# A causal attention layer solved block by block: the solve moved to the natural layout, with side work placed in the change of tiles

## The reference

```python
logits = jnp.einsum('bhqd,bhkd->bhqk', q, k) * scale
causal_mask = jnp.triu(jnp.full((s, s), -jnp.inf, dtype=logits.dtype), 1)
probs = jax.nn.softmax(logits + causal_mask, axis=-1)
L = jnp.eye(s, dtype=probs.dtype) - jnp.tril(probs, -1)
rhs = jnp.diagonal(probs, axis1=-2, axis2=-1)[..., None] * v
A = jax.scipy.linalg.solve_triangular(L, rhs, lower=True)
attn_output = A.transpose(0, 2, 1, 3).reshape(b, s, HID)
return attn_output @ Wd.T + bd
```

## Time and profile before

| what | us |
|---|---|
| median of 3 runs | 1500.24 (1497.93 to 1505.37) |
| profiled execution, its own span | 1507.1 |
| the steady part of the causal layer, solving 16 tiles | 462 (from 719 to 1181) |
| PE, DVE, ACT, POOL busy in these 462 us | 410, 232, 182, 147 |
| granted TensorE clock in these 462 us, mean | 0.87 |

### The profile page before, as it was taken

One profiled execution on the slowest core, in us unless ns is written; L12 is line 12 of the kernel. 1 busy time (PEld: TensorE's weight loads), 2 busy tenths in 40 slices (PEclk: granted clock), 3 DMA queues, 4 the chain that ended last, 5 costly groups with the idle time before them and its releaser, 6 DMA issues. The chain is left out here.

```text
span 1507.1 us, 30851 instructions
## 1 busy us (share of the span) xinstructions
PE 1237.4 (82%) x11642; PEld 673.8 (45%) x11642; DVE 1035.0 (69%) x2290; ACT 729.2 (48%) x1596; POOL 628.0 (42%) x838
## 2 busy tenths in 40 slices
PE   6656677779999988538889988988988799999976
PEld 2212232222333337424666766666666333333276
DVE  6699999979888955457446646645632588988653
ACT  3834334317766675313524523533442166676754
POOL 2279888853424215314423423223332524351244
PEclk9878888869999998758889879978997599999988
DMA  5378833023224022441421231141120231331213
GB/s 166 145 274 320 298 139 140 20 67 87 55 65 122 13 82 63 100 86 23 88 38 25 45 74 28 21 100 18 18 51 10 67 79 31 97 89 45 81 48 88
DMA packets 137737, 128.41 MB, mean 85 GB/s; under 512 B 92007, under 2 KB 123559, under 8 KB 132202
## 3 DMA queue, kind: packets, MB, share of 16 engines
q1 hardware_dynamic: 129536, 118.56, 28.6%
q0 software_dynamic: 2496, 5.13, 1.1%
q10 hardware_dynamic: 5558, 2.76, 0.9%
HBM read 105.61 MB, written 38.62 MB: 96 GB/s over the span
## 5 line engine op out<-in xcount | busy, mean ns | idle before, releaser
L1393 DVE TENSOR_REDUCE f_row_min<-f_ps 128x1 f32<-128x512 f32 x512 | 323.9, 676 | 55.6 <-PE f_ps L1720 55.2
L1283 ACT ACTIVATE f_e<-f_ps 128x512 f32<-128x512 f32 x512 | 282.8, 602 | 126.4 <-PE f_ps L1740 122.5
L1720 PE MATMUL f_ps<-f_operands 72*128 72x512 bf16 x512 | 205.4, 410 | 26.4 <-DMA f_operands<-k_scr 15.4
L1740 PE MATMUL f_ps<-f_operands 75*128 75x512 bf16 x512 | 189.5, 380 | 2.6 <-ACT f_e L1283 2.1
L790 PE MATMUL m_ps<-m_shared,sb_ident 128*128 128x512 f32 x256 | 136.8, 683 | 58.1 <-DVE m_shared L630 58.0
L363 POOL TENSOR_TENSOR m_drive<-m_du,m_ring 128x1024 f32<-128x1024 f32 x64 | 149.7, 2352 | 56.2 <-DVE m_ps L622 37.6
L495 ACT ACTIVATE m_ps<-m_delta,m_A 128x511 f32<-128x511 f32 x128 | 83.0, 681 | 131.7 <-DVE m_ps L622 109.0
L1751 PE MATMUL f_ps<-f_e,f_v_op 128*32 128x512 f32 x1024 | 136.4, 604 | 2.1 <-ACT f_e L1283 1.4
L2714 DVE TENSOR_TENSOR d_aT<-d_ps,d_aT 128x16 f32<-128x16 f32 x224 | 37.9, 169 | 140.9 <-PE d_ps L2892 140.7
L1720 PEld LDWEIGHTS f_ps<-f_operands 72*128 72x128 bf16 x512 | 51.3, 101 | 181.2 <-DVE f_row_min L1393 127.3
L2545 DVE TENSOR_REDUCE d_row_min<-d_ps 128x1 f32<-128x384 f32 (+3 forms) x176 | 106.3, 634 | 35.9 <-PE d_ps L2786 34.7
(11 more groups left out here) (298 smaller groups left out, 2345.3 us busy)
## 6 DMA issues: line engine op xcount, KB each, us to landing
m_ring<-bc_scr SPq DMA_DIRECT2D x32, 1024.0 KB, 5.4
f_rows_scr<-blank SPq DMA_DIRECT2D x2, 8707.5 KB, 30.8
f_wall<-f_wall SPq DMA_DIRECT2D x16, 578.0 KB
f_operands<-q_scr SPq DMA_DIRECT2D x32, 288.0 KB
f_operands<-k_scr SPq DMA_DIRECT2D x96, 96.0 KB
d_q_op<-q_scr SPq DMA_DIRECT2D x6, 576.0 KB
d_k_op<-k_scr SPq DMA_DIRECT2D x18, 192.0 KB
f_operands<-f_rows_scr SPq DMA_DIRECT2D x46, 64.5 KB, 1.8
```

The source lines that it names most:

```text
L1283: nc.scalar.activation(e_sb[:, n % 3, hh, :], ps[:, SCORE[(b * UNITS + u) % SCORE_BANKS], :], ACT.Exp, scale=SCALE).then_inc(s["e_out"], 1)
L1393: nc.vector.tensor_reduce(row_min[:, b % 2, u // TPB, u % TPB:u % TPB + 1], ps[:, MAXQ[(b * UNITS + u) % MAX_BANKS], :], AX.X, ALU.max, ne ...
L1720: nc.tensor.matmul(ps[:, MAXQ[n % MAX_BANKS], :], q_op(b, QK)[:, hd, t * P:(t + 1) * P], k_op(b, QK)[:, hd, :], start=True, stop=True).the ...
L1740: nc.tensor.matmul(ps[:, SCORE[n % SCORE_BANKS], :], k_op(b, QKS)[:, hd, t * P:(t + 1) * P], q_op(b, QKS)[:, hd, :], start=True, stop=True ...
```

## The change

All of it is in `delta_phase` and the two arrays it loads.

- **Natural layout.** The solution is held in `a_all` with tokens on partitions from the first product on. `product` now takes 32 columns of `mT` as the stationary operand and 8 columns of `a_all` as the moving one, and writes to `ps[own, ...]` with `own = token_group(k)`, one set of 32 PSUM partitions for all eight heads. For an odd k, where the block is the second of its group of 32 tokens, only the 16 rows of the block before are multiplied, and DVE multiplies by a column of zeros and ones (`second`) while it adds. `added` adds 32 x 64 numbers to `a_all` in place. The transposes of `aT` and ACT's copies into `a_nat` between steps are gone; one pair is left after `inverse` (`natural`, and ACT's `turned`).
- **The output** of a tile, two matmuls with `aT` before, is now a copy to `a_flat` (ACT), a transpose (`turn_out`, PE), a copy to `a_out` (ACT) and one matmul (L2938 in the changed kernel).
- **Side work.** Pieces 0 to 3 stand in the change of tiles. Pieces 4 to 13 follow ten of the 14 half-steps. After the half-steps (0, 1), (0, 2), (0, 4) and (0, 6) nothing stands.
- `mT` is computed for 112 of its 128 columns, since the first block needs none.

```diff
-PADDED = NH * HEAD_COLS + 2 * HD
+PADDED = HD + NH * HEAD_COLS
+CHANGE_HOOKS = 4
+HALF_STEPS = [(half, k) for k in range(1, BLKS) for half in range(2)]
+FOLLOWED = [i for i, (half, k) in enumerate(HALF_STEPS) if half or k not in (1, 2, 4, 6)]
+HOOK_AFTER = {i: CHANGE_HOOKS + place for place, i in enumerate(FOLLOWED)}
...
+        def token_group(k):
+            return slice(k // 2 * 2 * BLK, (k // 2 + 1) * 2 * BLK)
...
@@ multiplied, ACT @@
-                    nc.scalar.copy(mT[:, n % 2, i * GROUP:(i + 1) * GROUP, :].rearrange("p h i -> p (h i)"),
-                                   act_bank("mt", n, i)).then_inc(s["act_out"], 1)
+                    nc.scalar.copy(mT[:, n % 2, i * GROUP:(i + 1) * GROUP, BLK:P],
+                                   act_bank("mt", n, i).rearrange("p (h i) -> p h i", h=GROUP)[:, :, BLK:P]).then_inc(s["act_out"], 1)
+
+                def flattened(n):
+                    act.wait_ge(s["at_sb"], 2 * BLKS * (n + 1))
+                    if n >= 1:
+                        act.wait_ge(s["act_out"], in_act("turned_out", n - 1))
+                    nc.scalar.copy(a_flat[:, :, :], every_own(a_all[:, n % TPB, :])).then_inc(s["flat_out"], 1)
...
@@ added, DVE @@
-                    own = slice(k * BLK, (k + 1) * BLK)
+                    rows = token_group(k)
+                    held = own_cols(a_all[rows, n % TPB, :], half)
                     dve.wait_ge(s["at_ps"], 2 * (n * BLKS + k) + half + 1)
-                    nc.vector.tensor_tensor(aT[:, n % 2, half, own], ps[:, STEP[half], own], aT[:, n % 2, half, own],
-                                            ALU.add).then_inc(s["at_sb"], 1)
+                    if k % 2 == 0:
+                        nc.vector.tensor_tensor(held, step_cols(half, rows), held, ALU.add).then_inc(s["at_sb"], 1)
+                    else:
+                        nc.vector.scalar_tensor_tensor(out=held, in0=step_cols(half, rows), scalar=vec(core, "second")[rows, :],
+                                                       in1=held, op0=ALU.mult, op1=ALU.add).then_inc(s["at_sb"], 1)
...
@@ PE @@
                 def product(n, half, k):
-                    pe.wait_ge(s["an_sb"], 2 * (n * BLKS + k - 1) + half + 1)
-                    own = slice(k * BLK, (k + 1) * BLK)
-                    rows = slice(0, k * BLK)
-                    side_by_side(half, a_nat[:, :], lambda hd: mT[rows, n % 2, hd, own], rows, own, s["at_ps"])
-
-                def turned(n, half, k):
-                    pe.wait_ge(s["at_sb"], 2 * (n * BLKS + k) + half + 1)
-                    if n >= 1 and k == 0:
-                        pe.wait_ge(s["an_sb"], 2 * BLKS * n - 1 + half)
-                    turn_half(half, aT[:, n % 2], s["an_ps"])
+                    if k == 1:
+                        pe.wait_ge(s["an_sb"], 2 * n + half + 1)
+                    else:
+                        pe.wait_ge(s["at_sb"], 2 * (n * BLKS + k - 1) + half + 1)
+                    own = token_group(k)
+                    rows = slice(0, own.start) if k % 2 == 0 else slice(own.start, own.start + BLK)
+                    for gl in range(2):
+                        for hh in range(GROUP):
+                            c = (gl * GROUP + hh) * HD
+                            last = nc.tensor.matmul(ps[own, STEP[half], c:c + HD], mT[rows, n % 2, head(half, gl, hh), own],
+                                                    own_dims(a_all[rows, n % TPB, :], head(half, gl, hh)), start=True, stop=True)
+                    last.then_inc(s["at_ps"], 1)
...
+                    for i, (half, k) in enumerate(HALF_STEPS):
+                        product(n, half, k)
+                        if i in HOOK_AFTER:
+                            beside(n, HOOK_AFTER[i])
```

## The result

The changed kernel takes 1614.3 us (median of 4 runs, 1612.6 to 1618.1) against 1500.7 for the kernel before (1497.9 to 1505.4): 1.073 times as long, interval 1.069 to 1.078. The forecast was 1514 and its range ended at 1550. The direction was right and the size wrong by 100 us.

What follows compares the result with a forecast made beforehand. PE was taken to bound the stage, busy 410 of 462 us. Terms of 100 - 7 - 49 - 13 - 11 - 4 - 4 - 3 + 1 + 1 + 6 gave +17, said as +14 on 1500.2: 1514 us, range 1474 to 1550.

Steps and rivals of the forecast that it cites:

- The product: Products on PE: all 16 instructions in one column group, 0.38 us more each at fast clock, 0.64 at slow: +100 us.
- Transposes, waits, output: On PE, 208 transposes go (-49 us), with them the wait for DVE's addition (-13); two output matmuls become one (-4).
- the change of tiles: Between tiles, pieces 0 to 3 stand between PE's transposes of gT and aT, so waits go: -11 us.
- Waits for additions: Sign that the forecast is right: PE's waits for DVE's additions in the stage fall under 8 us.
- mT: The mT matmuls on PE, 112 of 128 columns in 64 groups: between -8 and 0 us, taken as -4.
- The clock: PE's granted clock may rise later in seven cold tiles, two mT groups each: half of 12 us taken, +6.
- the mean clock below 0.80: Sign for the clock case: PE's mean granted clock over the stage, 0.87 before, falls below 0.80.
- Those by tile: Signs in tile lengths: tile 7 about 27 us, tiles 2, 6 and 10 shorter by one to three, 5 and 9 longer.
- the clock stays down: Rival: PE's lighter work holds the clock at 0.5 for another 60 us, +28 or so, 1543 us; chance 0.17.
- priced "at nothing": In the product, the moving operand's fall from 16 columns to 8 was taken to change no time; weights count.
- 225 for both: DVE's addition after each product was to grow from 0.169 us to 0.225, mostly hidden behind PE: +1 us.

Runs made afterwards that it cites:

- filler: Two useless bf16 matmuls of 384 columns ahead of each product, results read by nobody: kernel before 1530.6 us, changed kernel 1633.3 us.

## Why the prediction was wrong

**The product** (+100): the unit prices were right, 0.60 and 0.96 us with starts 0.033 us apart. The total, +96.5 us over 14 tiles, is near by luck. I had 58 of 224 half-steps at half clock and it was 143; the pairs and the vanished waits made up for it.

**Transposes, waits, output** (-49, -13, -4) **and the change of tiles** (-11): right together, -64.4 us over 14 tiles. Waits for additions are under 1 us on PE where I said under 8. Taking the four pieces back cost 9 to 14 us, at overlapping intervals.

**mT** (-4): the sign was wrong, +39.8 us over 14 tiles, through the clock. Nor did the columns save anything: in tile 7 at full clock, with filler in both kernels, the four mT groups hold PE for 3.8 us with 112 columns and for 3.7 with 128.

**The clock** (+6): the step that failed. I priced it as two mT groups in each of seven tiles that were cold already, and held that the side work of the fast tiles would keep them at 1.00. Tile 7 fell to 0.70, and time at half clock rose by some 265 us, from 123 to 389. With all other terms as priced, this one should have been about +100; the estimate from tiles at equal clock puts it at some 77 or more. Of the prediction's signs, the mean clock below 0.80 is the one that came. Those by tile can't be read, since the ends of the stretches moved; from gathering to gathering tile 2, which was to be shorter, is 9 us longer. The rival "the clock stays down" named the mechanism and its point (fast tiles fall too), and was sized at 60 us more of half clock, 28 us of time. Why the clock stays down for so long, 15.4 us in tile 6 with PE never idle, no run takes apart.

What I had in hand and did not use: a moving operand of 8 columns in place of 16 was priced "at nothing". For the product's own length that is right, and in the old layout with one column group it cost 40 us (1579 to 1619) elsewhere. The length of the product cost clock too: one column group alone took time at half clock from 123 to 179 us.

**Open.** The old layout with one group and 8 columns has 0.76, the changed kernel with transposes put back 0.68. Between them stand fewer rows in the product (16 to 96 in place of up to 112), other waits and the places; no run parts these. What it is in 8 moving columns or in a longer product that lowers the clock stays open as well. How the 44 us of the places in the old layout divide between waits and clock is shown only as 25 us that filler does not take away.

## What to carry over

The granted clock of a stretch is a price. When an edit makes PE's instructions longer, or its operands narrower, at the same length, ask of every stretch around it whether it still runs at the level it ran at, and price the whole stretch at the other level as a rival of full size. To find what a change costs apart from the clock, put the same filler into both kernels and compare stretches at full clock in both, between the same two points of the work, and ask what the filler hides in waits. And a layout which needs fewer steps between engines can lose to one that keeps four column groups busy.

## What the runs showed of the hardware that I had not expected

- The granted clock fell after PE had been busy for 4.00 of 4.00 us and stayed at half while it was busy for 15.37 of 15.37, and halving the moving columns of 16-instruction products, with their length unchanged at 0.60 us, took the stage from 0.83 to 0.76.
- Two matmuls of 384 bf16 columns ahead of each product held the clock of the kernel before at 0.98 and brought that of the changed one to 0.80, but 128 x 128 float32 transposes at the same place did not lift the changed kernel's (0.66 to 0.68).
- Two column groups halve the distance between the starts of a product's instructions: on average 0.033 us with one group, 0.017 with two, 0.009 with four at full clock; 0.055, 0.027 and 0.014 at half.
- DVE's addition with a per-partition factor costs more than a plain one of the same shape. Rows of the changed kernel (count, busy us, mean ns), where I had 225 for both:

```profile
L2747 DVE SCALAR_TENSOR_TENSOR d_a_all<-d_ps,sb_vec,d_a_all 32x64 f32<-32x64 f32 x128 | 35.6, 280 | 132.2 <-PE d_ps L2986 131.5
L2745 DVE TENSOR_TENSOR d_a_all<-d_ps,d_a_all 32x64 f32<-32x64 f32 x96 | 20.0, 221 | 51.4 <-PE d_ps L2986 50.6
```
